# Quantised first-layer activations on VectorE, one of two ternary roundings on VectorE, a new order of the first norms and keys, and a last unit in halves

## The chip, the cores and the metric

The kernel runs on one core of a Trainium2 chip. The metric is the device time of one execution in microseconds; the time before is the median of three runs. A core has five engines with an instruction queue each: TensorE (PE in the views; PEld is its weight load), VectorE (DVE), ScalarE (ACT), GpSimd (POOL), and SyncE (SP), which here issues every DMA. An engine runs its queue in order; engines wait for each other through semaphores.

## What is computed

Two layers over 2 x 1024 tokens of width 256, each with gated cross-attention to 77 context rows (16 heads of 16) and a gated feed-forward part. In layer 0 the latter is ternary: activations are rounded to 8 bits, weights to -1, 0 or 1. In layer 1 the attention has a distance bias, and the feed-forward part is expert 0 of a mixture with a norm behind it.

```python
def _quant_act(x):
    scale = 127.0 / jnp.clip(jnp.max(jnp.abs(x), axis=-1, keepdims=True), EPS, None)
    xq = jnp.clip(jnp.round(x * scale), -128.0, 127.0) / scale
...
x = x + jnp.tanh(g_xattn[0]) * _L0_xattn_ref(_layernorm(x), ctx, w_q, w_k, w_v, w_o)
x = x + jnp.tanh(g_ffn[0]) * _L0_ffn_ref(_layernorm(x), w1, w2)      # _quant_act on x, and on gelu(h)
x = x + jnp.tanh(g_xattn[1]) * _L1_xattn_ref(_layernorm(x), ctx, ctx, distances, ...)
x = x + jnp.tanh(g_ffn[1]) * _L1_ffn_ref(_layernorm(x), ...)         # x + expert 0, normed
```

## The kernel before

The 2048 tokens are cut into 8 units (NU) of 256 rows; a tile holds a unit as 2 x 128 rows. Each engine's program is written out by hand as one function, so that its queue is the order of the code; semaphores (`then_inc`, `wait_ge`) tie the queues together. Two instructions that follow each other on VectorE or GpSimd with a dependence are tied by `link`.

**Start.** VectorE takes the statistics of units 0 and 1 (`ln0_stats`), norms them (`refine`, `ln0_apply`) and builds the key tables: `split_keys` makes high and low parts and the masked copies `km`, `keys_high` expands one (batch, half) of them to all heads (`kt_hi`, four calls). TensorE projects the keys (`tables_k`), transposes the normed units (`ln0_transposes`), projects queries (`queries`) and values (`tables_v`). SyncE loads inputs, then sends `km` into the tile `ktb` (`key_blocks`, three DMAs), then small rows of weights broadcast to all partitions (seven DMAs), then the query blocks and the shift rows of unit 0 into `qb`.

**Attention.** `attn_slot(l, s)` on each engine works on several units at once, in six steps r: maxima of the scores of unit s (`maxima` on TensorE, L1109 on VectorE), which end in the shift rows `mT` (L1522 on TensorE, L695 on ScalarE); scores, exponentials and their high parts on ScalarE (L704, L713) and low parts on GpSimd (`plo`, L491) for unit s-1; values for unit s-2; division, projection and residual for unit s-3; statistics (VectorE), factors (GpSimd, `factors_act`) and norm (ScalarE, L677) for unit s-4. In layer 0 unit s-4 is then quantised: `quantise` on VectorE (L1035 to L1042) takes the absolute maximum and its reciprocal at r = 4, just ahead of the last maximum of the slot, and `rounded` on ScalarE (L686) scales and rounds the unit at the end of the slot, just ahead of L695. Slots 0 to 3 also hold the first norms of the remaining units (`ln0_steps`, `ln0_applied`).

**Ternary stage.** Slots 9 to 12 of attention 0 also take ternary units 0 to 3; then follow ternary slots 4 to 8 alone, and 9 to 11 beside the first slots of attention 1. Per unit: a product to 1024 columns (L1600), gelu into the one buffer `h32` (L769), absolute maximum per half (L1155) and reciprocal (L1161) on VectorE, the rounding of the two halves of 128x1024 on ScalarE (L791, from `h32` to `hq`), transposes (L1615), their copies (L777), the second product (L1634), residual and statistics (L1178, L865), and GpSimd's norm (L431, L433, L517). The gelu of the next unit waits for both roundings. VectorE also builds the value tables of layer 1 here (`tables_v(1, step)`, L928 and L931, in slots 4 to 7) and the key tables (`keys_high(1, i)`).

**End.** `expert_hidden` and `expert_out` give a unit's sum in one PSUM bank; `expert_sum` adds and takes statistics on VectorE, GpSimd gives the factors, `expert_norm` (L1218, L1222) the output, which SyncE stores. GpSimd's queue per unit is: `xgb` (L527), `xnk` plus bias (L531, semaphore `xb`, which the sum waits for), factors.

## Time and profile before

| | us |
|---|---|
| runs | 415.22, 416.18, 414.89 (median 415.22) |
| profiled execution, its own time | 416.79 |
| its span, first to last instruction | 415.0 |
| TensorE busy / VectorE busy | 328.2 / 297.2 |
| ScalarE busy / GpSimd busy | 283.5 / 227.9 |

The span is that of one core; all times in the views count from its first instruction. Busy time is the union of an engine's instructions; waiting on a semaphore isn't counted, but an instruction that is held up after its issue by another engine is, so that its duration grows. The granted clock of TensorE is a share of 2.4 GHz, either 1.00 or 0.50 (1.2 GHz); in a stretch it is a mean.

### The profile page before, as it was taken

Reading aid. Unit: us, or ns where it says so; the run is one execution under the profiler, and the core shown is the slowest. Engines: PE = TensorE matmul, PEld = TensorE weight load, DVE = VectorE, ACT = ScalarE, POOL = GpSimd, SP = SyncE. Lnnn points to the kernel's source line nnn. Section 1 sums busy time; section 2 is a strip of 40 time slices with the busy share of each in tenths; the row PEclk is TensorE's granted clock in tenths of the full one; section 3 lists DMA queues with packets and bytes.
Section 4 is the critical chain, followed back from the end, with each engine's and each line's share of the span. In section 5 each row is a group of like instructions: output and inputs, shape, how many; then the busy total and the mean of one; then the engine's idle time right before and its main releaser. Section 6 shows DMA issues by size and latency. Waiting matters only on the chain.

```text
span 415.0 us, 8997 instructions
## 1 busy us (share of the span) xinstructions
PE 328.2 (79%) x3254; PEld 267.5 (64%) x3254; DVE 297.2 (72%) x690; ACT 283.5 (68%) x516; POOL 227.9 (55%) x408
## 2 busy tenths in 40 slices
PE   3658859787876765877787899898878899999990
PEld 2437648566664443455565788687667799888880
DVE  6685747877886657989986467777856558777775
ACT  4137787899896777988953788866678755555520
POOL 5246555776577411456766655567774155544442
PEclk9695898999899869869998999999999999999997
DMA  8996303111100000310073112211100000000001
GB/s 247 243 165 190 77 26 81 38 40 41 42 3 20 2 0 2 52 23 2 2 227 75 49 51 51 51 37 30 37 2 2 2 2 26 28 28 27 25 27 51
DMA packets 23171, 22.02 MB, mean 53 GB/s; under 512 B 4695, under 2 KB 22488, under 8 KB 23051
## 3 DMA queue, kind: packets, MB, share of 16 engines
q1 hardware_dynamic: 23128, 21.45, 20.9%
q8 instruction: 26, 0.43, 0.5%
q14 instruction: 17, 0.14, 0.1%
HBM read 10.34 MB, written 2.10 MB: 30 GB/s over the span
## 4 chain that ended last, share of the span: by engine, by line
PE 38%; DVE 26%; ACT 16%; issue 9%; POOL 8%; DMA 1%; SPq 0%; ACTq 0%; DVEq 0%; POOLq 0%
PE psA L1681 9%; PE psD L1666 4%; PE psBE L1666 4%; DVE st L865 4%; ACT pp_hi L713 3%; POOL lns L399 3%; DVE ham L1155 3%; PE psD L1370 3%; DVE mx L1109 3%; PE psA L1463 2%; ACT p L704 2%; PE psBE L1396 2%; PE psA L1634 2%; POOL pp_lo L491 1%; DVE o L1094 1%
## 5 line engine op out<-in xcount | busy, mean ns | idle before, releaser
L491 POOL TENSOR_TENSOR pp_lo<-p,pp_hi 124x512 f16<-124x512 f32 x80 | 92.7, 1178 | 45.6 <-ACT pp_hi L713 45.6
L399 POOL TENSOR_TENSOR lns<-lns,mhalf 128x2 f32<-128x2 f32 x40 | 32.2, 805 | 117.0 <-DVE lns L870 116.8
L1109 DVE TENSOR_REDUCE mx<-psBE 128x6 f32<-128x462 f32 (+1 forms) x96 | 54.6, 582 | 31.1 <-PE psBE L1396 30.8
L704 ACT ACTIVATE p<-psD 124x512 f32<-124x512 f32 x80 | 47.6, 597 | 28.7 <-PE psD L1370 26.1
L1370 PE MATMUL psD<-qb,ktb 98*124 98x256 f16 (+1 forms) x256 | 50.1, 293 | 5.7 <-DMA qb<-mT 4.8
L713 ACT ACTIVATE pp_hi<-p 124x512 f16<-124x512 f32 x80 | 50.4, 629 | 0.0
L1370 PEld LDWEIGHTS psD<-qb,ktb 98*124 98x124 f16 (+1 forms) x256 | 33.5, 147 | 10.5 <-DMA qb<-mT 6.8
L1396 PE MATMUL psBE<-kt_hi,q_hi 128*128 128x154 f16 (+2 forms) x160 | 34.2, 283 | 5.0 <-ACT mT L695 3.8
L1681 PE MATMUL psA<-ew_lo,pp_hi 128*128 128x256 f16 x128 | 34.9, 273 | 0.0
L1681 PE MATMUL psA<-ew_hi,pp_lo 128*128 128x256 f16 x128 | 34.9, 273 | 0.0
L1681 PE MATMUL psA<-ew_hi,pp_hi 128*128 128x256 f16 x128 | 34.9, 273 | 0.0
L1198 DVE TENSOR_TENSOR pp_lo<-space,pp_hi 128x512 f16<-128x512 f32 x32 | 23.4, 750 | 15.5 <-ACT space L815 15.4
L1422 PE MATMUL psA<-vo,pp_hi 124*128 124x34 f16 (+1 forms) x320 | 27.4, 181 | 8.8 <-ACT pp_hi L713 5.6
L1422 PEld LDWEIGHTS psA<-vo,pp_hi 124*128 124x128 f16 x320 | 25.4, 96 | 12.7 <-issue 12.4
L813 ACT ACTIVATE pp_hi<-psD,b1s 128x256 f16<-128x256 f32 x32 | 15.7, 490 | 19.8 <-PE psD L1666 19.8
L1425 PE MATMUL psA<-vo,pp_lo 124*128 124x34 f16 (+1 forms) x320 | 27.3, 181 | 0.0
L1424 PE MATMUL psA<-vlo,pp_hi 124*128 124x32 f16 (+1 forms) x320 | 27.3, 180 | 0.0
L865 DVE BATCH_NORM_STATS2 st<-xs 128x6 f32<-128x256 f32 x64 | 23.9, 415 | 2.3 <-DMA xs<-in_x 2.0
L1424 PEld LDWEIGHTS psA<-vlo,pp_hi 124*128 124x128 f16 x320 | 25.0, 96 | 0.4
L1425 PEld LDWEIGHTS psA<-vo,pp_lo 124*128 124x128 f16 x320 | 25.0, 96 | 0.0
L1367 PE MATMUL psD<-bb,selb 128*124 128x256 f16 x80 | 21.9, 284 | 1.2 <-DMA qb<-mT 1.1
L1396 PEld LDWEIGHTS psBE<-kt_hi,q_hi 128*128 128x128 f16 x160 | 15.3, 103 | 10.1 <-issue 4.6
(201 smaller groups left out, 1013.1 us busy)
## 6 DMA issues: line engine op xcount, KB each, us to landing
qb<-q_hi SPq DMA_DIRECT2D x32, 128.0 KB
xs<-in_x SPq DMA_DIRECT2D x8, 256.0 KB, 4.6
tw_raw<-in_tw SPq DMA_DIRECT2D x2, 1024.0 KB, 11.7
qb<-q_lo SPq DMA_DIRECT2D x16, 128.0 KB
space<-in_ew SPq DMA_DIRECT2D x2, 1024.0 KB, 6.5
out<-space SPq DMA_DIRECT2D x8, 256.0 KB, 2.1
ktb<-km SPq DMA_DIRECT2D x6, 248.0 KB, 9.4
qb<-bT_lo SPq DMA_DIRECT2D x8, 104.0 KB
```

The costliest lines, as they stand in the source:

```text
L399: nc.gpsimd.tensor_tensor(lns[:, n % 4, 1, :], lns[:, n % 4, 0, :], mhalf[:, :], ALU.pow).then_inc(s_rs, 1)
L491: nc.gpsimd.tensor_tensor(pl[:, u % 2, 2 * r:2 * r + 2, :], p32[:, n % 4, :, :], ph[:, u % 2, 2 * r:2 * r + 2, :], ALU.subtract).then_inc( ...
L704: a_(p32[:, n % 4, :, :], psD[n % 2][0:KR, :].rearrange("p (t r) -> p t r", t=2), ACT.Exp, scale=1.0 / SSC).then_inc(a["exp"], 1)
L713: a_(ph[:, u % 2, 2 * r:2 * r + 2, :], p32[:, n % 4, :, :], ACT.Copy).then_inc(a["phi"], 1)
L865: i = v.bn_stats(st[:, n % 4, j, :], src[:, j, :])
L1109: v.tensor_reduce(pairs[:, MP[k][0]:MP[k][1]:MP[k][2], :], psBE[:, n % 2, 0:hn * KEYS].rearrange("p (q e k) -> p q e k", e=2, k=KEYS), AX. ...
L1370: i = mm(o, ktbf[0:rows, block(g, hf * B + b, t):block(g, hf * B + b, t) + KR], qb[0:rows, u % NQ, g, hf, :], start=first, stop=(k == 1 an ...
L1396: i = mm(psBE[:, n % 2, o0 * KEYS:(o0 + c1 - c0) * KEYS], q[0][:, u % 2, hf, j * 128:(j + 1) * 128], kt[:, hf, b, c0 * KEYS:c1 * KEYS], st ...
L1422: mm(o, p_, w.rearrange("p s c -> p (s c)"), start=(hf == 0 and t == 0), stop=False, skip_group_check=True)
L1424: mm(ov[:, :, 0:HD], p_, wl, start=False, stop=False, skip_group_check=True)
L1425: i = mm(o, pl[:, u % 2, hf * TPH + t, rows_], w.rearrange("p s c -> p (s c)"), start=False, stop=(hf == 1 and t == TPH - 1), skip_group_c ...
L1681: i = mm(o, ehT[x_][:, u % 2, c, j * 128:(j + 1) * 128], ew2[w_][:, c, :], start=(j == 0 and c == 0 and x_ == 0 and w_ == 0), stop=(j == 1 ...
```

## The change

1. **Activations rounded by VectorE.** `rounded` on ScalarE goes. `quantise` rounds the unit by two instructions of 128x256 behind its reciprocal, ahead of the scales (`dq1`) and of the slot's last maximum.
2. **Ternary rounding.** Of the two halves, ScalarE keeps j = 0; VectorE does j = 1 (128x1024) in `ternary_first` behind the reciprocal, with a semaphore `q1b` of its own.
3. **Start.** On VectorE the head masks come first, both norms ahead of the keys, then two of four `keys_high`, then the masked copies (`keys_masked`, cut out of `split_keys`), the statistics of unit 2, and the low queries; the other two `keys_high` go to slots 2 and 3. TensorE projects queries 0 ahead of the transposes of unit 1. ScalarE spreads the query weights ahead of the key tables. SyncE sends the seven rows ahead of the key blocks.
4. **Layer-1 tables.** Value table steps go from ternary slots 4 to 7 to 7 to 10, without the column of ones (L931), which layer 0 has written; `keys_high(1, i)` for i = 1, 2, 3 go from slots 4, 5, 6 to 4, behind 9 and behind 10.
5. **End.** The last unit is summed, normed and stored in halves of 128 rows, the first half as soon as its product is done; its second half uses another PSUM bank.

VectorE at the start, from the first norm on; before:

```order
L884 TENSOR_SCALAR xn<-xs,mv,lns 128x256 x2
L958 TENSOR_REDUCE hmask<-id 128x8
L960 TENSOR_REDUCE pmask<-hmask 128x2
L896 CAST ksp_hi<-k 128x308
L897 TENSOR_TENSOR ksp_lo<-k,ksp_hi 128x308
L901 TENSOR_SCALAR km<-ksp_hi,pmask 128x4x77 x2
L901 TENSOR_SCALAR km<-ksp_lo,pmask 128x4x77 x2
L876 TENSOR_TENSOR lns<-lns 128x2
L877 TENSOR_TENSOR lns<-lns 128x2
L878 TENSOR_SCALAR lns<-lns 128x2
L879 TENSOR_TENSOR lns<-lns 128x2
L884 TENSOR_SCALAR xn<-xs,mv,lns 128x256 x2
```

after:

```order
L891 TENSOR_SCALAR xn<-xs,mv,lns 128x256 x2
L883 TENSOR_TENSOR lns<-lns 128x2
L884 TENSOR_TENSOR lns<-lns 128x2
L885 TENSOR_SCALAR lns<-lns 128x2
L886 TENSOR_TENSOR lns<-lns 128x2
L891 TENSOR_SCALAR xn<-xs,mv,lns 128x256 x2
L903 CAST ksp_hi<-k 128x308
L904 TENSOR_TENSOR ksp_lo<-k,ksp_hi 128x308
L921 TENSOR_TENSOR kt_hi<-ksp_hi,hmask 128x616 x2
L911 TENSOR_SCALAR km<-ksp_hi,pmask 128x4x77 x2
L911 TENSOR_SCALAR km<-ksp_lo,pmask 128x4x77 x2
L872 BN_STATS st<-xs 128x6 x2
```

The second norm (xn) stands ahead of the keys (ksp, kt_hi, km), and two expansions stand ahead of the masked copies.

VectorE in slot 4 of attention 0, the quantisation of unit 0; before:

```order
L1035 TENSOR_REDUCE am<-xn 128x2
L1037 TENSOR_SCALAR am<-am 128x1 x2
L1040 RECIPROCAL am<-am 128x2
L1042 TENSOR_SCALAR dq<-am,ws 128x1 x2
L1109 TENSOR_REDUCE mx<-psBE 128x2x2
L1079 SCALAR_TENSOR_TENSOR q_lo<-psA,q_hi 128x512
L1066 SCALAR_TENSOR_TENSOR xs<-psA,gsc,xs 128x512
```

after:

```order
L1048 TENSOR_REDUCE am<-xn 128x2
L1050 TENSOR_SCALAR am<-am 128x1 x2
L1052 RECIPROCAL am<-am 128x2
L1055 TENSOR_SCALAR xn<-xn,am 128x256 x2
L1058 TENSOR_SCALAR dq<-am,ws 128x1 x2
L1125 TENSOR_REDUCE mx<-psBE 128x2x2
L1095 SCALAR_TENSOR_TENSOR q_lo<-psA,q_hi 128x512
L1082 SCALAR_TENSOR_TENSOR xs<-psA,gsc,xs 128x512
```

Two instructions that round xn stand between the reciprocal and the last maximum of the slot.

VectorE at the end, from the sum of the unit before the last on; before:

```order
L1207 SCALAR_TENSOR_TENSOR space<-tw_raw,psA 128x512
L865 BN_STATS st<-space 128x6 x2
L868 BN_AGGR mv<-st 128x2 x2
L870 TENSOR_SCALAR lns<-mv 128x2
L1218 SCALAR_TENSOR_TENSOR space<-space,mv,bc 128x256 x2
L1222 SCALAR_TENSOR_TENSOR space<-space,lns 128x256 x2
L1207 SCALAR_TENSOR_TENSOR space<-tw_raw,psA 128x512
L865 BN_STATS st<-space 128x6 x2
L868 BN_AGGR mv<-st 128x2 x2
L870 TENSOR_SCALAR lns<-mv 128x2
L1218 SCALAR_TENSOR_TENSOR space<-space,mv,bc 128x256 x2
L1222 SCALAR_TENSOR_TENSOR space<-space,lns 128x256 x2
```

after:

```order
L1226 SCALAR_TENSOR_TENSOR space<-tw_raw,psA 128x512
L872 BN_STATS st<-space 128x6 x2
L875 BN_AGGR mv<-st 128x2 x2
L877 TENSOR_SCALAR lns<-mv 128x2
L1242 SCALAR_TENSOR_TENSOR space<-tw_raw,psA 128x256
L1243 BN_STATS st<-space 128x6
L1244 BN_AGGR mv<-st 128x2
L1245 TENSOR_SCALAR lns<-mv 128x1
L1264 SCALAR_TENSOR_TENSOR space<-space,mv,bc 128x256 x2
L1268 SCALAR_TENSOR_TENSOR space<-space,lns 128x256 x2
L1242 SCALAR_TENSOR_TENSOR space<-tw_raw,psA 128x256
L1243 BN_STATS st<-space 128x6
```

The first half-sum of the last unit stands ahead of the norm of the unit before it (two rows of space<-space), and the second behind it; the two half-norms follow.

The diff, cut to its core:

```diff
@@ -335,11 +335,11 @@
             sp.dma_start(tw1_raw[:, :, :], io["tw1"].rearrange("(c p) n -> p c n", p=128)).then_inc(d_tw1, 16)
-            key_blocks(0)
...
                 sp.dma_start(o, io[name].to_broadcast([128, o.shape[1]])).then_inc(d_row, 16)
+            key_blocks(0)
@@ -371,12 +371,16 @@
                 shift_rows(1, u)
-            for u in range(NU):
+            for u in range(NU - 1):
...
                              y32[:, u % 2, :, :]).then_inc(d_out[u % 2], 16)
-            for i in (0, 1):
-                sp.wait_ge(d_out[i], 16 * NU // 2)
+            u = NU - 1
+            for j in (0, 1):
+                sp.wait_ge(E["out"], u + 1 + j)
+                sp.dma_start(io["out"][u * UR + j * 128:u * UR + (j + 1) * 128, :], y32[:, 1, j, :]).then_inc(d_out[1], 16)
+            sp.wait_ge(d_out[0], 16 * NU // 2)
+            sp.wait_ge(d_out[1], 16 * (NU // 2 + 1))
@@ -424,6 +428,18 @@
+
+            def factors_half(j):
+
+                n = 5 * NU - 1
+                g = lns[:, n % 4, :, j:j + 1]
+                pool.wait_ge(s_var, n + 1 + j)
+                nc.gpsimd.tensor_tensor(g[:, 1, :], g[:, 0, :], mhalf[:, 0:1], ALU.pow).then_inc(s_rs, 1)
+                pool.wait_ge(s_rs, n + 1 + j)
+                link(nc.gpsimd.tensor_tensor(g[:, 2, :], g[:, 1, :], g[:, 1, :], ALU.mult))
+                link(nc.gpsimd.tensor_tensor(g[:, 3, :], g[:, 0, :], g[:, 2, :], ALU.mult))
+                link(nc.gpsimd.tensor_scalar(g[:, 4, :], g[:, 3, :], -0.5, 1.5, ALU.mult, ALU.add))
+                nc.gpsimd.tensor_tensor(g[:, 5, :], g[:, 4, :], g[:, 1, :], ALU.mult).then_inc(E["fac"], 1)
@@ -530,7 +546,10 @@
                                         orow[:, 1:2, :].to_broadcast([128, 2, D]), ALU.add).then_inc(E["xb"], 1)
-                factors_dve(4 * NU + u, E["fac"])
+                if u < NU - 1:
+                    factors_dve(4 * NU + u, E["fac"])
+            for j in (0, 1):
+                factors_half(j)
@@ -592,11 +611,10 @@
             keys_spread(0)
-            tables_k(0)
...
             a_(spreaded(wqp), spread(wraw[0, "q"]), ACT.Copy).then_inc(s_wqp, 1)
+            tables_k(0)
             ln0_transposed(0)
-            ln0_transposed(1)
@@ -747,8 +756,6 @@
                         expert_hidden(s - NU - 1, (r - 2, r - 1))
-                if l == 0 and 0 <= s - 4 < NU:
-                    rounded(s - 4)
@@ -784,12 +792,10 @@
                 if u < NU:
-                    for j in (0, 1):
-                        n = 2 * u + j
-                        act.wait_ge(f["amax"], u + 1)
-                        ge(act, f["phT"], n - 3)
-                        a_(hq[u % 2][:, j, :], h32[:, j, :], ACT.Identity, scale=ham[:, 2, j:j + 1],
-                           bias=epsc[:, 4:5]).then_inc(f["q1"], 1)
+                    act.wait_ge(f["amax"], u + 1)
+                    ge(act, f["phT"], 2 * u - 3)
+                    a_(hq[u % 2][:, 0, :], h32[:, 0, :], ACT.Identity, scale=ham[:, 2, 0:1],
+                       bias=epsc[:, 4:5]).then_inc(f["q1"], 1)
@@ -895,6 +902,9 @@
+
+            def keys_masked(l):
@@ -951,17 +962,19 @@
             v.memset(ktb[:, :, :, :].rearrange("p n g k -> p (n g k)").bitcast(F32), 0.0).then_inc(s_bm, 1)
-            ln0_stats(0)
-            ln0_stats(1)
-            ln0_apply(0, refine(0, SX))
...
             link(v.tensor_reduce(pmask[:, :], hmask[:, :].rearrange("p (g r) -> p r g", r=2), AX.X, ALU.max))
+            ln0_stats(0)
+            ln0_stats(1)
+            ln0_apply(0, refine(0, SX))
+            ln0_apply(1, refine(1, SX))
             split_keys(0)
-            ln0_apply(1, refine(1, SX))
-            for i in range(4):
+            for i in range(2):
                 keys_high(0, i)
+            keys_masked(0)
+            ln0_stats(2)
@@ -970,10 +983,10 @@
-                if (s, r) in ((0, 2), (0, 3), (0, 5), (1, 1), (1, 5), (2, 1)):
-                    ln0_stats({(0, 2): 2, (0, 3): 3, (0, 5): 4, (1, 1): 5, (1, 5): 6, (2, 1): 7}[s, r])
-                if (s, r) == (0, 1):
-                    queries_lo(0, 0)
+                if (s, r) in ((0, 2), (0, 5), (1, 1), (1, 5), (2, 1)):
+                    ln0_stats({(0, 2): 3, (0, 5): 4, (1, 1): 5, (1, 5): 6, (2, 1): 7}[s, r])
+                if (s, r) in ((2, 3), (3, 4)):
+                    keys_high(0, s)
@@ -1036,8 +1049,11 @@
                 link(i)
-                ge(dve, a["q1"], u)
                 v.reciprocal(am[:, 2, :], am[:, 1, :]).then_inc(a["xn"], 1)
+                dve.wait_ge(a["xn"], u + 1)
+                for j in (0, 1):
+                    i = v.tensor_scalar(xn[:, u % 2, j, :], xn[:, u % 2, j, :], am[:, 2, j:j + 1], MAGICQ, ALU.mult, ALU.add)
+                i.then_inc(a["q1"], 1)
@@ -1157,15 +1173,18 @@
                     link(i)
-                    ge(dve, f["q1"], 2 * u)
+                    ge(dve, f["q1"], u)
                     v.reciprocal(g[:, 2, :], g[:, 1, :]).then_inc(f["amax"], 1)
+                    dve.wait_ge(f["amax"], u + 1)
+                    ge(dve, f["phT"], 2 * u - 2)
+                    v.tensor_scalar(hq[u % 2][:, 1, :], h32[:, 1, :], g[:, 2, 1:2], MAGICQ, ALU.mult, ALU.add).then_inc(f["q1b"], 1)
...
                         v.tensor_scalar(dq2[:, n:n + 1], g[:, 1, j:j + 1], ws[:, 1:2], gate[:, 2:3], ALU.mult, ALU.mult)
-                if 4 <= s < 8:
-                    if s == 4:
+                if 7 <= s < 11:
+                    if s == 7:
                         dve.wait_ge(A[0]["ppv"], 2 * NU)
-                    tables_v(1, s - 3)
+                    tables_v(1, s - 6)
@@ -1209,6 +1228,33 @@
+            def expert_sum_half(j):
+                e, u = E, NU - 1
+                n = 4 * NU + u
+                y = y32[:, u % 2, j, :]
+                if j == 0:
+                    dve.wait_ge(e["half"], 1)
+                    dve.wait_ge(e["xb"], u + 1)
+                    dve.wait_ge(d_out[u % 2], 16 * (u // 2))
+                else:
+                    dve.wait_ge(e["pm2"], u + 1)
+                acc = acc_(u)[:, 0:D] if j == 0 else psX[:, D:2 * D]
+                link(v.scalar_tensor_tensor(y, xnk[:, 2 * u + j, :], SY / SX, acc, ALU.mult, ALU.add))
+                link(v.bn_stats(st[:, n % 4, j, :], y))
+                link(v.bn_aggr(mv[:, n % 4, j, :], st[:, n % 4, j, :]))
+                v.tensor_scalar(lns[:, n % 4, 0, j:j + 1], mv[:, n % 4, j, 1:2], EPS * SY * SY, None,
+                                ALU.add).then_inc(s_var, 1)
+
+            def expert_norm_half(j):
+                e, u = E, NU - 1
+                n = 4 * NU + u
+                y = y32[:, u % 2, j, :]
+                dve.wait_ge(e["fac"], u + 1 + j)
+                link(v.scalar_tensor_tensor(y, y, mv[:, n % 4, j, 0:1], gg[:, :], ALU.subtract, ALU.mult))
+                dve.wait_ge(e["xgb"], u + 1)
+                v.scalar_tensor_tensor(y, y, lns[:, n % 4, 5, j:j + 1], xgb[:, u % 2, j, :],
+                                       ALU.mult, ALU.add).then_inc(e["out"], 1)
@@ -1232,18 +1279,21 @@
                     split_keys(1)
+                    keys_masked(1)
...
                 ternary_slot(s)
-                if s < 7:
-                    keys_high(1, s - 3)
+                if s == 4:
+                    keys_high(1, 1)
...
             ternary_slot(NU + 1)
+            keys_high(1, 2)
...
             ternary_slot(NU + 2)
+            keys_high(1, 3)
@@ -1264,9 +1314,12 @@
                 expert_hidden(u, (2, 3))
-            for u in (NU - 2, NU - 1):
-                expert_sum(u)
-                expert_norm(u)
+            expert_sum(NU - 2)
+            expert_sum_half(0)
+            expert_norm(NU - 2)
+            expert_sum_half(1)
+            for j in (0, 1):
+                expert_norm_half(j)
@@ -1341,7 +1394,6 @@
             ln0_transposes(0)
-            ln0_transposes(1)
@@ -1637,8 +1689,8 @@
                     pe.wait_ge(f["xn"], u + 1)
-                    if u < 4:
-                        pe.wait_ge(s_vo, 8 + 2 * u + 1)
+                    if 3 <= u < 7:
+                        pe.wait_ge(s_vo, 8 + 2 * (u - 3) + 1)
@@ -1674,17 +1726,21 @@
                 ge(pe, e["y"], u - 1)
+                last = u == NU - 1
                 for j in (0, 1):
-                    o = acc_(u)[:, j * D:(j + 1) * D]
+                    o = (psX if last and j == 1 else acc_(u))[:, j * D:(j + 1) * D]
...
                             i = mm(o, ehT[x_][:, u % 2, c, j * 128:(j + 1) * 128], ew2[w_][:, c, :],
-                                   start=(j == 0 and c == 0 and x_ == 0 and w_ == 0),
-                                   stop=(j == 1 and c == FK - 1 and x_ == 1))
+                                   start=((last or j == 0) and c == 0 and x_ == 0 and w_ == 0),
+                                   stop=((last or j == 1) and c == FK - 1 and x_ == 1))
+                    if last and j == 0:
+                        i.then_inc(e["half"], 1)
...
             queries(0, 0)
+            ln0_transposes(1)
```

## Rows read from the trace of the kernel before

**Rows 1.** The page: span, and busy time, share of the span and instructions by engine.

```profile
span 415.0 us, 8997 instructions
PE 328.2 (79%) x3254; PEld 267.5 (64%) x3254; DVE 297.2 (72%) x690; ACT 283.5 (68%) x516; POOL 227.9 (55%) x408
```

**Rows 2.** Stretches: us, busy us (instructions) by engine, clock, DMA share, GB/s.

```profile
83.00:95.00 12.00, 10.11 (x131) 8.29 (x126) 9.10 (x24) 11.03 (x22) 8.74 (x13) 1.00 0.12 35
188.00:196.00 8.00, 5.98 (x62) 4.38 (x61) 7.83 (x21) 7.09 (x8) 5.23 (x9) 1.00 0.01 2
```

**Rows 3.** Timeline, 0 to 42 us: start, us, engine, line, operation, out<-in, [idle before <-releaser].

```profile
14.28 1.12 PE L1284 MATMUL psA<-id,xn 128*128 128x128 f32 x4 [4.13 <-DVE xn L884]
15.19 3.62 PE L1463 MATMUL psA<-xTf,ew_lo 128*128 128x256 f32 x8
21.51 1.19 DVE L1109 TENSOR_REDUCE mx<-psBE 128x6 f32<-128x462 f32 x2 [4.45 <-PE psBE L1396]
29.61 1.54 SPq L323 DMA_DIRECT2D qb<-mT  x2
33.18 0.85 PE L1370 MATMUL psD<-qb,ktb 98*124 98x256 f16 x3
```

**Rows 4.** DMA issues, first 60 us: KB each, median us to landing.

```profile
ktb<-km SPq DMA_DIRECT2D x3, 248.0 KB, 13.3
```

**Rows 5.** Stretches of 2 us in the start.

```profile
16.00:18.00 2.00, 2.00 (x6) 1.60 (x5) 1.07 (x2) 0.03 (x1) 0.00 (x0) 0.50 1.06 345
28.00:30.00 2.00, 1.14 (x9) 0.84 (x10) 1.63 (x5) 1.77 (x4) 1.59 (x6) 1.00 0.76 163
```

**Rows 6.** Timeline of ScalarE, slot 4 of layer 0.

```profile
79.22 1.09 ACT L677 ACTIVATE xn<-xs,lns 128x256 f32<-128x256 f32 x2 [1.36 <-POOL lns L416]
81.88 1.08 ACT L686 ACTIVATE xn<-xn,epsc,am 128x256 f32<-128x256 f32 x2
82.87 0.45 ACT L695 ACTIVATE mT<-psBE,epsc 16x256 f16<-16x256 f32 x1
```

**Rows 7.** Timeline of VectorE, the same slot.

```profile
80.34 0.69 DVE L1035 TENSOR_REDUCE am<-xn 128x2 f32<-128x512 f32 x1 [1.53 <-ACT xn L677]
81.62 0.47 DVE L1109 TENSOR_REDUCE mx<-psBE 128x4 f32<-128x308 f32 x1
```

**Rows 8.** Timeline of GpSimd, the same slot.

```profile
79.14 4.51 POOL L491 TENSOR_TENSOR pp_lo<-p,pp_hi 124x512 f16<-124x512 f32 x4
```

**Rows 9.** Timelines of GpSimd and VectorE, slot 3 of layer 0.

```profile
63.59 2.32 POOL L491 TENSOR_TENSOR pp_lo<-p,pp_hi 124x512 f16<-124x512 f32 x2 [0.77 <-ACT pp_hi L713]
...
63.88 1.02 DVE L996 TENSOR_SCALAR bc<-bc,gate 128x256 f32<-128x256 f32 x1
64.82 1.25 DVE L997 TENSOR_SCALAR bc<-bc,gate 128x256 f32<-128x256 f32 x1
70.07 0.34 DVE L999 TENSOR_SCALAR orow<-orow,gate 128x256 f32<-128x256 f32 x1
```

**Rows 10.** Timeline of VectorE, the fourth ternary unit.

```profile
172.48 2.35 DVE L1155 TENSOR_REDUCE ham<-space 128x1 f32<-128x1024 f32 x2 [0.63 <-ACT space L769]
```

**Rows 11.** Timelines of VectorE and GpSimd, ternary slots 4 and 5.

```profile
187.37 0.79 DVE L911 TENSOR_TENSOR kt_hi<-ksp_hi,hmask 128x616 f16<-128x616 f16 x1
191.77 0.80 DVE L931 TENSOR_SCALAR vo<-vm 124x15 f16<-124x15 f32 x1
...
191.24 1.27 POOL L517 TENSOR_TENSOR xs<-xs,orow 128x512 f32<-128x512 f32 x1
```

**Rows 12.** Timelines of TensorE and VectorE, ternary slots 6 and 9.

```profile
195.34 0.43 PE L1329 MATMUL psA<-vsp_hi,selb 77*124 77x48 f16 x5 [1.03 <-DVE xTf L890]
...
221.52 0.88 DVE L1178 SCALAR_TENSOR_TENSOR xs<-psA,dq,xs 128x256 f32<-128x256 f32 x2 [1.50 <-PE psA L1634]
```

**Rows 13.** Timelines of GpSimd and VectorE, the end.

```profile
404.71 1.44 POOL L531 TENSOR_TENSOR tw_raw<-tw_raw,orow 128x512 f32<-128x512 f32 x1
...
411.52 0.88 DVE L1222 SCALAR_TENSOR_TENSOR space<-space,lns 128x256 f32<-128x256 f32 x2
```

29 lines of the change are left out of this document (13 added, 16 removed).

## Prediction

> **What bounds the kernel now.** I read the page first: in a span of 415.0 us no engine is busy throughout; TensorE has 79%, VectorE 72%, ScalarE 68%, GpSimd 55% [rows 1]. So the price of an edit depends on its stage, and I read busy time by stretch, then the chain of work that ended last. In slot 5 of the first attention layer ScalarE works 11.03 of 12 us and VectorE 9.10; in ternary slots 5 and 6 VectorE works 7.83 of 8 us [rows 2]. There the timelines say who comes last. The experts of layer 1 (322 to 405 us) are a wall of TensorE work which the change leaves alone except for its last unit. The change acts in four places: the start, the first attention layer from slot 4 on, the ternary stage, and the end.
>
> **The start.** TensorE waits 4.13 us for the second norm before its transposes at 14.28, then does the first queries in 3.62 us, at half clock (granted 0.50, that is 1.2 GHz, after it had stood still; 1.00 is 2.4 GHz), and VectorE idles 4.45 us until the first maxima at 21.51 [rows 3, 5]. Now the queries stand before the second transposes, the second norm before the key tables, two of four key expansions are put off to slots 2 and 3 (VectorE idle there in the before trace), and one statistics step and the low queries stand ahead of slot 0. VectorE's list up to the first maximum then ends at about 16.5, and slot 0 starts some 5 us earlier. What is late next is the transfers. Today the first shift rows are sent at 29.61 and the first scores run at 33.18 [rows 3]. The scores also need the key blocks and the query blocks. The key blocks are now sent behind seven row transfers; today they take 13.3 us to land [rows 4], since the DMA engines are full to 28 us and still at 0.76 until 30 [rows 5]. The same bytes are queued ahead of the first scores in either order, so these can't start before about 30. That gains 33.2 - 30.2 = 3.0 us, plus about 0.3 for a wait on VectorE that has gone by then. **Term 1: -3.3** (bounds -4.8 and -1).
>
> **Rounding of the first-layer activations.** Per unit, ScalarE loses two instructions (1.08 us [rows 6]), and VectorE gets two of 128x256 between its reciprocal and the last maximum of the slot. Free, such an instruction takes 0.34 (L999, [rows 9]), the pair 0.65. In slot 4 the chain is: norm on ScalarE at 79.22, absolute maximum at 80.34, reciprocal ends at 81.5, last maximum at 81.62; the shift (L695) waits at 82.87 for the rounding in front of it [rows 6, 7]. Without other waits the new chain ends the last maximum at 82.75 and the shift starts near 83.1: +0.3. The ScalarE time that is freed is thus not gained, as VectorE's chain is nearly as long.
> But GpSimd then runs four subtractions in a row, 79.14 to 83.65, 1.13 each [rows 8]. Rows 9 show what happens to this very kind of instruction: L996 is issued at 63.88 and ends at 64.90, when the first of two GpSimd subtractions (63.59 to 65.91, a border near 64.75) is done; L997, right behind it, ends at 66.07, after the second. Each takes 0.29 to 0.34 when GpSimd is idle. So of a pair each instruction waits for one GpSimd operation. In slot 4 the first waits for 82.52, the second for 83.65: last maximum at 84.5, shift at 84.8, +1.9. The same reading gives +1.1 in slot 5, -0.55 in slot 6 (GpSimd's row has ended, ScalarE's relief counts), +1.9 in slot 7, where VectorE carries the chain, and +0.95 in slot 8, where part of the wait is only moved. Sum with waits +5.3; without any +1.0; if ScalarE's time came back in slots 5 and 6 as well, -1. I take a value near the upper end, as L996, L997 and L931, which meet a GpSimd operation, all wait for it [rows 9, 11]. **Term 2: +4.3** (-1 to +5.3).
> The Trainium skill, page "SBUF — State Buffer", section "Who interferes with whom", states that VectorE and GpSimd share a port pair as an exclusive lock: an instruction of VectorE in a two-port mode and one of GpSimd exclude each other, and the later one blocks fully until the other has ended. By that rule this term is the +5.3 and not the +1.0. The trace agrees: 1.25 us for L997 against 0.34 for L999.
>
> **Ternary rounding of the second half, slots 9 to 12.** One of two ScalarE roundings of 128x1024 goes to VectorE, about 0.75 free. In slot 9 the halves run beside each other and the unit's own new work is paid back (-0.3). In slot 10 the rounding stands before the statistics, whose GpSimd factors and ScalarE norm follow: about +1.0. In slot 11 VectorE has the activations' rounding and the half, 1.4 us, against 0.63 idle before its next maximum at 172.48 [rows 10]: another +0.8 to +1.0. In slot 12 VectorE has no gap at all: +0.75. **Term 3: +2.5** (0 to +4).
>
> **Ternary slots 4 to 8.** Here VectorE sets the pace [rows 2]. Taken off: in slots 4 to 6 the value tables (two of 0.32, and L931, which takes 0.80 because GpSimd's L517 runs from 191.24 to 192.51: 1.34 in all), in 5 and 6 also the key expansion, 0.71 net [rows 11]. Added: the half, 0.75 free to 1.8 behind a GpSimd operation; I take 1.35. That gives -1.0 in slot 4 (a gap of 0.86 goes too), -0.7 each in 5 and 6, +0.6 in 7, -0.1 in 8. **Term 4: -2.0** (-5 to -0.3).
>
> **Ternary slots 9 and 10, beside attention slots 0 and 1 of layer 1.** Two of the table steps land here: TensorE has 0.7 more (L1329, ten matmuls) ahead of a product for which VectorE already waits 1.50 us, and VectorE an expansion of 0.7 ahead of the next maxima [rows 11, 12]. Some is hidden by waits for transfers. **Term 5: +1.2** (0 to +2.5).
>
> **The end.** The last unit's sum, norm and output go in halves; half 0 is ready on TensorE 2.6 us before half 1. But the first half-sum needs GpSimd's L531 of the last unit, which ends at 404.71 + 1.44 = 406.15 [rows 13], behind the factors of the unit before. VectorE now waits there with that unit's norm queued behind it. From about 405.8: half-sum 1.15, norm 1.75 to 2.3, half-sum 1.15, factors 1.9, half-norm 0.9: VectorE ends at 412.4 to 413.1, today at 411.52 + 0.88 = 412.4 [rows 13]; the last transfer is half as large. **Term 6: +0.1** (-0.8 to +0.8).
>
> **Sum.** -3.3 + 4.3 + 2.5 - 2.0 + 1.2 + 0.1 = +2.8 us. The profiled execution took 416.79 (span 415.0 and 1.8 around it), 1.6 above the median; I put the difference on the median: 415.2 + 2.8 = **418.0**.
>
> **Rivals.** (a) *Balance.* The waits on GpSimd hit only about half of the roundings, since the shorter start shifts the phases, and ScalarE's relief counts in slots 5 and 6: term 2 is near +1.5, the sum 0.0: 415.2. For it: slot 6 meets no GpSimd work. Against: GpSimd's row starts with the factors that also release the norm, so both keep step. (b) *Faster.* The roundings don't wait (another operation and another tile than L996), term 2 +0.5, term 3 +1, term 4 -4, term 1 -4, the others +0.5 and 0: -6 at the far end, about -3.5 where half of that comes: 411.7. For it: the instructions at 76.5 and later that round weights take their free time; ScalarE loses some 2 us per unit where it is busiest. Against: rows 9. (c) *Clearly slower.* The key blocks, put behind seven transfers, land later than the queries and the shift rows: the start gains nothing from 30.2 on, the price is 3 us, and it decides if the first scores start after 33. Then 418.0 + 3.3 = 421.3. For it: 13.3 us to land. Against: the same bytes are ahead of the first scores anyway.
>
> **How the numbers follow.** Forecast 0.45 (own range 416.5 to 420), (a) 0.20, (b) 0.27, (c) 0.08. About 0.3%, or 1.25 us, is what a measurement of this kernel can tell from no change. Faster: (b) and an edge of (a), 0.29. Within: most of (a), 0.20. Slower: the forecast and (c), 0.51. The range 411.5 to 421.0 leaves out the far ends of (b) and (c).
>
> **What would show it.** First scores at 30 to 31 (term 1); each pair of the new 128x256 roundings spread over 1.5 to 2.3 us in slots 4, 5, 7 and 8, beside GpSimd's subtractions (term 2); ternary slots 5 and 6 near 7.0 us instead of 7.7 (term 4); VectorE idle for 3 to 4 us before the first half-sum (term 6). Pairs of 0.65 would refute term 2, and with it the sign.

## The result and the profile after

| | before | after |
|---|---|---|
| runs | 415.22, 416.18, 414.89, 414.37 | 427.6, 431.98, 427.48, 427.97 |
| median, us | 415.06 | 427.79 |
| profiled execution / its span | 416.79 / 415.0 | 427.6 / 425.8 |

The changed kernel is slower: ratio 1.033, 95% interval 1.026 to 1.040. The forecast was 418.0 (411.5 to 421.0): the sign was right, the size far too small. Of the executions behind all numbers below, four that were over 1.5% longer than the fastest of their kernel, at a low granted clock, are left out of medians and ratios: one of g1 (435.37), two of g3 (419.84, 416.42) and one of the kernel before (420.10). The rows below answer [rows 1, 2]: slot 5 is within a microsecond of its old place, ternary slots 5 and 6 begin five later.

```profile
span 425.8 us, 8995 instructions
PE 330.2 (78%) x3254; PEld 269.5 (63%) x3254; DVE 310.7 (73%) x712; ACT 267.4 (63%) x492; POOL 232.6 (55%) x413
...
83.00:95.00 12.00, 9.87 (x104) 8.06 (x103) 9.20 (x25) 9.93 (x19) 8.11 (x12) 0.94 0.16 35
193.00:201.00 8.00, 7.25 (x59) 5.04 (x58) 7.79 (x19) 6.35 (x8) 5.84 (x12) 0.96 0.01 2
```

VectorE is busy 13.5 us longer, ScalarE 16.1 less, and the span is 10.8 longer. In slot 5 ScalarE works 9.93 of 12 us instead of 11.03; in the ternary slots VectorE still works 7.79 of 8.

To see where, I compared the start of the same instruction in both traces. Each number is the delay against the profiled execution of the kernel before, in us; the right columns are experiments below (each named by its label's first part), which change the kernel before by one or two parts.

| moment | after | e5 round | f1 half | f2 tables | g4 half + tables | g3 start, no ones |
|---|---|---|---|---|---|---|
| shift rows, slot 3 | -3.3 | +0.6 | -0.5 | 0.0 | +0.6 | -1.5 |
| absolute maximum, slot 9 | +3.1 | +6.8 | -0.2 | +0.6 | +0.6 | -1.4 |
| residual, ternary unit 1 (slot 12) | +6.2 | +7.3 | +1.4 | +1.2 | +2.7 | -1.6 |
| residual, unit 5 (ternary slot 7) | +4.1 | +6.3 | +4.3 | -2.0 | +0.5 | -4.6 |
| residual, unit 6 (ternary slot 8) | +7.1 | +6.3 | +6.1 | +2.6 | +5.2 | -3.9 |
| shift rows, slot 2 of layer 1 | +10.6 | +6.3 | +4.8 | +6.1 | +8.6 | -5.2 |
| end of the span | +10.8 | +6.4 | +4.9 | +6.2 | +8.6 | -5.1 |

After slot 2 of layer 1 the delay stays the same to the end in every kernel: what is lost before it is never won back.

**Start.** The timeline of the changed kernel, which answers [rows 3]:

```profile
25.56 1.54 SPq L323 DMA_DIRECT2D qb<-mT  x2
...
30.95 0.90 PE L1422 MATMUL psD<-qb,ktb 98*124 98x256 f16 x3 [1.93 <-DMA qb<-mT]
```

The shift rows go out 4.1 us earlier, the first scores run 2.2 us earlier, and they wait for the landing of the shift rows, not of the key blocks (those take 8.8 us now).

**Activations' rounding.** Timeline of VectorE (and one row of GpSimd) in slots 4 to 8; L1055 is the new pair:

```profile
75.84 4.54 POOL L507 TENSOR_TENSOR pp_lo<-p,pp_hi 124x512 f16<-124x512 f32 x4
...
78.20 2.33 DVE L1055 TENSOR_SCALAR xn<-xn,am 128x256 f32<-128x256 f32 x2
...
92.81 0.67 DVE L1055 TENSOR_SCALAR xn<-xn,am 128x256 f32<-128x256 f32 x2
...
105.46 0.62 DVE L1055 TENSOR_SCALAR xn<-xn,am 128x256 f32<-128x256 f32 x2
...
116.91 2.33 DVE L1055 TENSOR_SCALAR xn<-xn,am 128x256 f32<-128x256 f32 x2
...
131.73 2.35 DVE L1055 TENSOR_SCALAR xn<-xn,am 128x256 f32<-128x256 f32 x2
```

Three pairs of eight are held up by 1.7 us; the others take their free 0.62 to 0.67. Within the first pair each instruction ends just behind one of GpSimd's borders, which lie 1.13 apart (75.84 + 3 x 1.13 = 79.24, + 4 x 1.13 = 80.38):

```profile
78.20 1.17 DVE L1055 TENSOR_SCALAR xn<-xn,am 128x256 f32<-128x256 f32 x1
...
79.30 1.24 DVE L1055 TENSOR_SCALAR xn<-xn,am 128x256 f32<-128x256 f32 x1
```

**Ternary slots 8 to 10 and the first slots of layer 1.** Timelines of TensorE and VectorE; L1382 are the table products, L1667 the transposes, L1686 the second product, L938 the table copies, L1337 the transposes of the norm:

```profile
207.04 0.44 PE L1382 MATMUL psA<-vsp_hi,selb 77*124 77x48 f16 x5 [4.80 <-DVE xTf L897]
...
214.96 0.43 PE L1382 MATMUL psA<-vsp_hi,selb 77*124 77x48 f16 x5 [2.20 <-DVE xTf L897]
...
215.51 1.05 PE L1667 MATMUL psA<-id,p 128*128 128x128 f16 x16
216.41 1.91 PE L1686 MATMUL psA<-ew_hi,wspace 128*128 128x256 f16 x16
...
214.12 0.69 DVE L897 TENSOR_TENSOR xTf<-psA,xTf 128x512 f16<-128x512 f32 x1
...
218.35 0.88 DVE L1197 SCALAR_TENSOR_TENSOR xs<-psA,dq,xs 128x256 f32<-128x256 f32 x2 [1.92 <-PE psA L1686]
...
242.15 0.40 DVE L938 TENSOR_TENSOR vlo<-psA,vm 124x240 f16<-124x240 f32 x1
...
242.65 0.63 PE L1337 MATMUL psA<-id,xn 128*128 128x128 f32 x4 [1.71 <-issue]
...
243.94 0.69 DVE L897 TENSOR_TENSOR xTf<-psA,xTf 128x512 f16<-128x512 f32 x1 [1.39 <-ACT xTf L580]
```

In the kernel before, ternary slot 8 had no table products, and its transposes ran as soon as ScalarE had rounded each half:

```profile
207.88 0.61 PE L1615 MATMUL psA<-id,p 128*128 128x128 f16 x8
208.80 0.62 PE L1615 MATMUL psA<-id,p 128*128 128x128 f16 x8 [0.31 <-ACT p L791]
209.26 1.91 PE L1634 MATMUL psA<-ew_hi,wspace 128*128 128x256 f16 x16
```

Its residual followed 3.28 us behind that of the unit before (207.93 to 211.21); now it is 6.28 (212.07 to 218.35). VectorE's half of unit 7 was rounded by 211.03 and ScalarE's by 212.15 (L797, 210.91 + 1.24), but the transposes start at 215.51: the table products stand ahead of them in the queue and wait, TensorE idle for 2.20 us, for VectorE's last copy (L897) out of the bank into which both the table products and the transposes of the norm go (psX). The slot thus runs through one chain, copy (L897), tables, transposes, ScalarE's copies, product, residual, where the kernel before had its transposes done by then.

**End.** VectorE, the last unit, answering [rows 13]:

```profile
411.95 0.17 DVE L877 TENSOR_SCALAR lns<-mv 128x2 f32<-128x2 f32 x1
416.50 0.42 DVE L1242 SCALAR_TENSOR_TENSOR space<-tw_raw,psA 128x256 f32<-128x256 f32 x1 [4.39 <-POOL tw_raw L547]
...
423.15 0.48 DVE L1255 SCALAR_TENSOR_TENSOR space<-space,lns 128x256 f32<-128x256 f32 x1
```

The idle time that the forecast named is there (4.39 us), and the end comes out even: +10.6 at slot 2, +10.8 at the end.

### The profile page after: what moved, and what is told of

Its sections match the earlier page's. It is cut to its first block, busy times and chain, and to the rows that moved or that the text cites. A ratio compares the mean times of both kernels' runs of the same rounds, so it can differ in the third digit from the quotient of the medians.

```text
span 425.8 us, 8995 instructions
## 1 busy us (share of the span) xinstructions
PE 330.2 (78%) x3254; PEld 269.5 (63%) x3254; DVE 310.7 (73%) x712; ACT 267.4 (63%) x492; POOL 232.6 (55%) x413
## 4 chain that ended last, share of the span: by engine, by line
PE 38%; DVE 30%; ACT 11%; issue 9%; POOL 8%; DMA 3%; SPq 1%; ACTq 0%; POOLq 0%; DVEq 0%
PE psA L1734 9%; PE psD L1718 4%; PE psBE L1718 4%; DVE ham L1171 4%; PE psD L1422 3%; DVE st L872 3%; DVE mx L1125 3%; ACT pp_hi L722 3%; POOL lns L403 2%; PE psA L1515 2%; DVE xn L1055 2%; PE psBE L1448 2%; DVE xs L1197 2%; PE psA L1520 2%; DMA qb<-mT 1%
## 5 line engine op out<-in xcount | busy, mean ns | idle before, releaser
L403 POOL TENSOR_TENSOR lns<-lns,mhalf 128x2 f32<-128x2 f32 x39 | 30.9, 792 | 110.7 <-DVE lns L877 110.5
L1422 PE MATMUL psD<-qb,ktb 98*124 98x256 f16 (+1 forms) x256 | 51.5, 301 | 5.4 <-DMA qb<-mT 4.7
L1422 PEld LDWEIGHTS psD<-qb,ktb 98*124 98x124 f16 (+1 forms) x256 | 33.9, 150 | 10.3 <-DMA qb<-mT 6.7
L819 ACT ACTIVATE pp_hi<-psD,b1s 128x256 f16<-128x256 f32 x32 | 15.7, 489 | 19.8 <-PE psD L1718 19.8
L1718 PE MATMUL psD<-xTf,ew_hi 128*128 128x256 f16 x128 | 21.4, 273 | 0.4 <-ACT p L713 0.4
```

Source lines behind the costliest of these rows:

```text
L403: nc.gpsimd.tensor_tensor(lns[:, n % 4, 1, :], lns[:, n % 4, 0, :], mhalf[:, :], ALU.pow).then_inc(s_rs, 1)
L1422: i = mm(o, ktbf[0:rows, block(g, hf * B + b, t):block(g, hf * B + b, t) + KR], qb[0:rows, u % NQ, g, hf, :], start=first, stop=(k == 1 an ...
L1718: i = mm(eps_(n)[:, i2 * UR:(i2 + 1) * UR], ew1[w_][:, k, c], x_[:, k, :], start=(i2 == 0 and k == 0 and x_ is xh and w_ == 0), stop=(i2 = ...
```

## The experiments

Ratios are to the kernel before on the same chip, with their 95% intervals. Runs were made in four groups, in which the median of the kernel before was 416.0, 417.5, 416.3 and 416.9, so I compare ratios, and delays of traces at the same instruction. "Part" is a part of the change.

### Undoing one part of the changed kernel

e3: part 4 undone, but L931 stays out. e2: part 2 undone. e1: part 1 undone.

```diff
 e3, TensorE (VectorE and keys_high likewise)
-                if 7 <= s < 11:
-                    tables_vo(1, s - 7)
+                if 4 <= s < 8:
+                    tables_vo(1, s - 4)
 e2, ScalarE rounds both halves
-                    v.tensor_scalar(hq[u % 2][:, 1, :], h32[:, 1, :], g[:, 2, 1:2], MAGICQ, ALU.mult, ALU.add).then_inc(f["q1b"], 1)
 e1, ScalarE
+                if l == 0 and 0 <= s - 4 < NU:
+                    rounded(s - 4)
```

> The changed kernel, with the value-table steps back in ternary slots 4 to 7 and the key expansions 1 to 3 of layer 1 back in slots 4 to 6 (the column of ones stays left out). Theory: in the changed kernel the table products stand on TensorE ahead of the transposes and the second product of ternary slots 7 to 10 and wait there for VectorE's copy of the norm before them (4.80, 2.20 and 0.28 us idle), and later the transposed norm waits for VectorE's table copies (242.65). That is the +6.5 between ternary slot 8 and attention slot 2 of layer 1. With the tables back this goes, and slots 4 to 6 pay about 1 to 2 us of VectorE's time again: 422.5 to 423.5, 4.5 to 5.5 under the changed kernel. Rival: the +6.5 is made by the rounding of the second half on VectorE (1.40 us at 209.63 instead of 0.75) and by what it pushes: then the tables' place matters little and the time stays at 427 to 429.

> The changed kernel, with both halves of the ternary rounding on ScalarE again. Theory: the rounding of the half costs 3 to 4 us, all in slots 9 to 12 of the first attention layer, where VectorE sets the pace; the time falls to 424 to 425. The +6.5 between ternary slot 8 and attention slot 2 of layer 1 stays. Rival: the half rounding is behind the +6.5 as well; then the time falls to 418 to 420.

> The changed kernel, with the rounding of the first-layer activations on ScalarE again. Theory: three of the eight pairs (slots 4, 7 and 8) stand still for 1.7 us each behind GpSimd's subtractions, and the pair in front of the last maxima costs some tenths in the other slots: the part costs 5 to 6 us, and the time falls to 422 to 423. Rival: other work takes the same places and only shifts the phases (the shorter start is given back anyway when the slots' phases move): the time falls by 2 us or less, to 426 or more.

Measured: e3 425.95, ratio 1.027 (1.020 to 1.034); e2 428.13, 1.033 (1.028 to 1.038); e1 423.62, 1.021 (1.015 to 1.028). All three expectations were put as if the parts were independent. e1 comes near, e2 gave nothing back, and e3 is split: two executions took 423.5 and 424.0 at a granted clock of 0.924, the changed kernel's own, near the 422.5 to 423.5 expected, and two, the profiled one among them, 427.9 and 429.0 at 0.914 and 0.915. In e1's trace the delay of the shift rows stays between -3.2 and -2.7 from slot 1 to slot 7, so what the changed kernel lost there (-3.7 to +1.9) is part 1's. In e3 the +3.0 of slot 8 is gone (+10.1 to +10.3), as the theory said, but slots 4 to 7 went from +7.5 to +10.1, where the changed kernel falls from +6.2 to +4.1. VectorE fills those slots without a gap; one of them, from one unit's absolute maximum at 196.09 to the next's at 204.11, is 8.0 us, against 7.1 in the changed kernel (199.66 to 206.81):

```profile
196.09 2.34 DVE L1171 TENSOR_REDUCE ham<-space 128x1 f32<-128x1024 f32 x2
...
198.92 0.92 DVE L1180 TENSOR_SCALAR p<-space,ham 128x1024 f32<-128x1024 f32 x1
...
203.40 0.79 DVE L921 TENSOR_TENSOR kt_hi<-ksp_hi,hmask 128x616 f16<-128x616 f16 x1
204.11 2.34 DVE L1171 TENSOR_REDUCE ham<-space 128x1 f32<-128x1024 f32 x2
```

So in slots 4 to 7 the half and the tables compete: with the tables back there, the half's time is paid in full. e2 shows no such filling. It gives back 2.0 us in slots 9 to 12 (+7.2 to +8.3, the changed kernel +3.1 to +6.2), its slots 4 to 7 fall from +8.3 to +6.1, as the changed kernel's do, and it loses in slot 8, +5.9, where its TensorE ran at half clock (0.50 from 217 to 223): from its table products to the end of the second product it took 6.35 us (216.87 to 223.22), and the changed kernel 3.36 at clock 1.00 (214.96 to 218.32). In attention slot 8 too, where neither part acts yet, e3 and e2 lose 3.2 and 3.5 us and the changed kernel 1.2; the granted clock from 120 to 140 us is 0.66 and 0.57 against 0.76. All four executions of e2 had a low clock (0.904 to 0.916; the changed kernel's four 0.916 to 0.924); whether that comes with this program or by chance is open. Undoing parts one by one didn't give their price; they had to be added one by one.

### One part alone on the kernel before

e4: part 3. e5: part 1. f1: part 2. f2: part 4. g4: parts 2 and 4. Their diffs are those lines of the change.

> The kernel before with only the new start (order of the first norms, keys, masks, queries, and of the row and key-block transfers). Theory: the gain at the first scores (3.3 us) is carried through to the end, since no later stage waits for a fixed moment: 411.5 to 412.5. Rival: the first attention layer gives part of it back (the two key expansions and the second copy of the norm now lie in slots 0 to 3, or other waits meet GpSimd's rows): 413.5 to 415.

> The kernel before with only the rounding of the first-layer activations moved to VectorE. Theory: the instructions stand still behind GpSimd's subtractions (up to 1.7 us for a pair, as at 78.20, 116.91 and 131.73 of the changed kernel, where a pair took 2.33 us instead of 0.62), and each pair delays the last maxima: 4 to 6 us, 419 to 421. Rival: the part costs its own 0.65 us per unit at most and often nothing; what was seen in the changed kernel came from the other parts: 415 to 417.

> The kernel before with only the second half of the ternary rounding moved to VectorE. The forecast's terms for it: +2.5 in slots 9 to 12, and about 1.35 us of VectorE's time per unit in ternary slots 4 to 8, where VectorE sets the pace, less what ScalarE's relief returns. Theory: with the table steps and the column of ones still in slots 4 to 7, the half comes on top of them in full: +2.5 and then 0.8 to 1.3 per slot, 421 to 424. Rival: the half is paid in slots 9 to 12 only and hidden later, since gelu and transposes of the next unit start earlier: 417 to 418.5.

> The kernel before with only the late layer-1 tables (value steps in ternary slots 7 to 10, expansions 2 and 3 behind slots 9 and 10, no column of ones). Theory: slots 4 to 6 get shorter by 0.7 to 0.9 each (VectorE sets the pace there), but from slot 8 on the table products stand ahead of the transposes on TensorE and wait for VectorE's copy of the norm, some 6 us in slot 8 and 9 when both roundings are ScalarE's, and 1 to 2 more where x transposes and the next maxima wait for the table copies and the expansion: 418 to 421. Rival: the late place is harmless when VectorE has no rounding to do, and the relief of slots 4 to 6 stays: 412.5 to 414.5.

> The kernel before with the second half of the ternary rounding on VectorE and the late layer-1 tables together (each alone cost 5.7 and 6.6 us). Theory: the table steps and expansions that leave slots 4 to 6 make room for the half there, and the half's halving of ScalarE's work shortens what waits behind the late tables in slots 8 and 9, so together they cost 6.5 to 8: 423 to 424.5. Rival: the costs are of different places and add up: 12 us, 427.5 to 429.

| | median | ratio, interval | part's cost, % |
|---|---|---|---|
| e4 start | 414.89 | 0.998 (0.995 to 1.002) | -0.2 |
| e5 rounding | 423.11 | 1.011 (1.006 to 1.015) | +1.1 |
| f1 half | 421.99 | 1.013 (1.008 to 1.017) | +1.3 |
| f2 tables | 422.93 | 1.014 (1.009 to 1.020) | +1.4 |
| g4 half and tables | 425.14 | 1.019 (1.017 to 1.022) | +1.9 |

e4 took its rival's time (413.5 to 415), not the 411.5 to 412.5 of the theory: its first scores come at 32.36, 0.8 earlier instead of 3, and its trace ends 2.0 earlier. e5's time is above the 419 to 421 expected, but in a group where the kernel before took 417.5; the cost of 4 to 6 held, by the median (5.6) and by the trace: pairs of 2.33 in slots 4, 7 and 8, and +6.2 between slot 3 and slot 9. f1's held: +2.9 of its delay arises in slots 4 to 7. For f2 I gave 418 to 421; it took 422.9, more than its rival and more than the theory. The relief in slots 4 to 7 is real (+1.2 to -2.0), and 8.1 us are lost behind it: 4.6 in slot 8, 3.5 until slot 2 of layer 1. Of the 4.6, a part is TensorE's clock, which in f2 fell to 0.51 and 0.64 from 209 to 213; the same transposes and product take 1.05 and 1.91 us in the changed kernel:

```profile
209.71 1.88 PE L1618 MATMUL psA<-id,p 128*128 128x128 f16 x16
211.38 2.44 PE L1637 MATMUL psA<-ew_hi,wspace 128*128 128x256 f16 x16
```

From the table products to the end of the second product f2 takes 4.99 us and g4, which loses 4.7 in this slot, 5.01 (clock 0.73 and 0.50 from 211 to 215), where the changed kernel takes 3.36. Less this difference, slot 8 costs 3.0 in f2, in g4 and in the changed kernel alike (in e2, too, 5.9 less 3.0 is 2.9).

g4 is between the theory (6.5 to 8) and the sum (12): 8.2 by medians. The two overlap by about 4.1 us by medians (8.2 against 5.7 + 6.6) and by 2.5 in the traces (8.6 against 4.9 + 6.2), where f1's lacks a half clock of 1.6 us that the others have between slots 0 and 1 of layer 1 (see the last section). 1.9 of it is in slots 4 to 7 (g4 -2.2 there, f1 and f2 together +2.9 - 3.2 = -0.3), 1.7 in slot 8 (g4 +4.7, f1 and f2 together +1.8 + 4.6). So the late tables do make room for the half, as the change seems to want, but they cost more later than they give. The parts now add up: start -2.0, rounding +6.4, half and tables +8.6, less 1.6 of half clock in g4's slot 8, are +11.4 by the traces, against +10.8; by ratios -0.2 + 1.1 + 1.9 = +2.8%, against +3.3 (2.6 to 4.0).

### The wait on GpSimd: form and size of the instruction

e6 writes the rounding with a second tensor operand, f4 cuts each rounding in two; both on e5.

```diff
 e6
-                    i = v.tensor_scalar(xn[:, u % 2, j, :], xn[:, u % 2, j, :], am[:, 2, j:j + 1], MAGICQ, ALU.mult, ALU.add)
+                    i = v.scalar_tensor_tensor(xn[:, u % 2, j, :], xn[:, u % 2, j, :], am[:, 2, j:j + 1],
+                                               epsc[:, 4:5].to_broadcast([128, D]), ALU.mult, ALU.add)
 f4
+                    for h in (0, 1):
+                        xq = xn[:, u % 2, j, h * 128:(h + 1) * 128]
+                        i = v.tensor_scalar(xq, xq, am[:, 2, j:j + 1], MAGICQ, ALU.mult, ALU.add)
```

> As the run before, but each rounding is written as one instruction with a second tensor operand (a broadcast constant, scalar_tensor_tensor instead of tensor_scalar). Theory: L1197, an instruction of this form and size, takes 0.44 us wherever GpSimd works beside it, so it is only the form with one tensor operand that is held up; each pair takes 0.9 us everywhere, none above 1.1, and the part costs 1.5 to 2.5 us: 416.5 to 418. Rival: every instruction of VectorE that comes then is held up (or slowed by the traffic): pairs of 2 us and more show as before, and the time is that of the run before or longer.

> The kernel before with the rounding of the first-layer activations on VectorE, each 128x256 instruction cut into two of 128x128 (same elements, four instructions instead of two). Theory: an instruction of this kind waits until the GpSimd operation in progress has ended, whatever its own size; four of them beside a row of GpSimd subtractions take up to four such waits, 3.4 to 4.6 us instead of 2.33 in slot 4, 7 and 8, and the time grows by 2 to 5 us: 425 to 428. Rival: the two engines share a rate, so the time goes with the elements: 2.4 to 2.7 us for the four, and 423 to 424.

e6 took 426.69, 1.021 (1.015 to 1.027); f4 427.55, 1.026 (1.019 to 1.033). e6's theory fell: the pair takes 2.60 us in slot 4 and 0.88 where it is free, so it is held up by the same 1.7.

```profile
81.54 2.60 DVE L1031 SCALAR_TENSOR_TENSOR xn<-xn,am,epsc 128x256 f32<-128x256 f32 x2
...
149.39 0.88 DVE L1031 SCALAR_TENSOR_TENSOR xn<-xn,am,epsc 128x256 f32<-128x256 f32 x2
```

L1197, on which I had built it, has this form too, but one of its operands lies in PSUM; here is its group in the changed kernel (min, median and max in ns), GpSimd working beside nine of the sixteen:

```profile
L1197 DVE SCALAR_TENSOR_TENSOR xs<-psA,dq,xs x16: 467/473/484, 173.2 to 229.6; 128x256 f32<-128x256 f32 x16
```

So the name of the operation doesn't tell whether it waits: with both tensor operands in SBUF it did, with one of them in PSUM it didn't. e6 took 3.6 us more than e5. The Trainium skill, page "SBUF — State Buffer", section "Who interferes with whom", states that an instruction of VectorE with two inputs in SBUF contends with a GpSimd instruction that reads SBUF, and one with at most one such input outside the two-port modes doesn't; the trace agrees with both halves, 2.60 against 0.88 us and 467 to 484 ns. That sentence stands beside the one that the prediction used.

f4 settles the price. GpSimd's row of four subtractions here runs from 78.77 to 83.27, with borders near 79.9, 81.0 and 82.1; VectorE's four quarters:

```profile
81.14 1.10 DVE L1033 TENSOR_SCALAR xn<-xn,am 128x128 f32<-128x128 f32 x1
...
82.16 1.19 DVE L1033 TENSOR_SCALAR xn<-xn,am 128x128 f32<-128x128 f32 x1
...
83.27 0.47 DVE L1033 TENSOR_SCALAR xn<-xn,am 128x128 f32<-128x128 f32 x2
```

The first two wait for one GpSimd operation each and take about as long as the full ones (1.17 and 1.24), at half the size; then the row ends and the other two are free. I had expected four waits, 3.4 to 4.6 us, and forgotten the row's end: 2.6. The time still went up, by 4.4 against e5's median (two runs only, and in another group: by ratios 1.5%), in the trace by 2.8; slot 5, where the pair had slipped through in 0.80, now takes 1.83.

### The late tables: order in TensorE's queue

e7 is the changed kernel with the table products behind the transposes; g1 is the changed kernel with the old start, g2 both.

```diff
+                ternary_transposed(s - 1)
                 if 7 <= s < 11:
                     tables_vo(1, s - 7)
-                ternary_transposed(s - 1)
```

> The changed kernel, with the value-table products of layer 1 behind the transposes of the same ternary slot on TensorE instead of ahead of them (slots 7 to 10). Theory: in slot 9 the transposes wait in the queue behind the table products, which wait until VectorE has copied the norm out of the same bank; without that the second product comes some 2 to 3 us earlier: 424.5 to 426. Rival: the transposes would wait for ScalarE or for the rounding anyway, and VectorE then waits for the tables instead, ahead of its residual: 427 to 429.

> The changed kernel with the start of the kernel before. Theory: all that the start gained, at its first scores, is lost again, no more: 1.5 to 3.5 us above the changed kernel, 429 to 431. Rival: the new start shifts phases against GpSimd's rows and is itself behind a part of the loss: below 428.

> As the run before, with the value-table products of layer 1 behind the transposes of the same ternary slot on TensorE instead of ahead of them. Theory: the transposes and the second product of slots 8 and 9, and the transposed norm in attention slot 2 of layer 1, come 2 to 3 us earlier in all: 2 to 3 us below the run before. Rival: no difference in time, since VectorE then waits for the tables in the same slots.

e7 427.45, 1.022 (1.016 to 1.028); g1 429.3, 1.030 (1.027 to 1.032); g2 428.51, 1.026 (1.023 to 1.029). e7's time is its rival's (427 to 429), though its ratio lies below the changed kernel's 1.033, with intervals that overlap. g2 is 0.8 below g1 by medians, with intervals that touch: the expected 2 to 3 us aren't there. In the traces slot 8 costs 2.1 instead of 3.0 in both pairs (e7 against the changed kernel, g2 against g1), so the order is a third of it. The rest stays, since the second product still stands behind the tables, which wait for the copy of the norm (e7):

```profile
215.30 1.06 PE L1667 MATMUL psA<-id,p 128*128 128x128 f16 x16
217.53 0.43 PE L1382 MATMUL psA<-vsp_hi,selb 77*124 77x48 f16 x5 [1.18 <-DVE xTf L897]
...
218.09 1.91 PE L1686 MATMUL psA<-ew_hi,wspace 128*128 128x256 f16 x16
```

That another bank would free it is argued from these waits; it wasn't tried. Much of each pair's remaining difference is the clock's. From the shift rows of slot 0 to those of slot 1 of layer 1, e7 and g1, whose TensorE stayed at 1.00, both take 12.3 us, and the changed kernel and g2, which fell to 0.50 (235 to 237, and 235 to 241), take 14.0 and 15.2. So e7, whose shift rows of slot 3 come 2.7 later than the changed kernel's, ends level with it (+10.9), and g2 ends 2.5 behind g1. g1's median is 1.5 above the changed kernel's 427.8, the low edge of its theory, but by ratios it is no higher (1.030 against 1.033), so these runs don't show what the start is worth there. Its rival, below 428, fell: the losses didn't grow from the new start.

### What is left when nothing moves onto VectorE

e8 and, once more in more rounds, g3: part 3 and the missing column of ones. f3 adds part 5.

```diff
-                i.then_inc(s_vo, 1)
-                v.tensor_scalar(vo[:, b, hf, :, :, HD], vm[:, :, :], SM * SONE, None, ALU.mult).then_inc(s_vo, 1)
+                i.then_inc(s_vo, 1 + l)
+                if l == 0:
+                    v.tensor_scalar(vo[:, b, hf, :, :, HD], vm[:, :, :], SM * SONE, None, ALU.mult).then_inc(s_vo, 1)
```

> The kernel before with the new start, and without the column of ones of the layer-1 value tables (L931, four times in ternary slots 4 to 7, 0.35 to 0.80 us each on VectorE), which layer 0 has written. Theory: VectorE sets the pace there, so the column's 1.5 to 3 us come off, on top of the start's 1.5: 411 to 412.5. Rival: VectorE then waits for TensorE's second product instead: 413.5 to 415.

> The kernel before with the new start, no column of ones in layer 1, and the end in halves: the three parts that moved no work onto VectorE. Theory: start 1.5 to 3, column 1 to 2, end nothing: 412 to 414, as without the halves at the end. Rival: the shorter last transfer and the earlier first half take 0.5 to 1.5 us off at the end: 411 to 412.

> The kernel before with the new start and no column of ones in layer 1, once more and in more rounds. Theory: 1.5 to 3.5 us under the kernel before, as in the first measurement of it (3.6 by medians). Rival: the first measurement met a fast transfer in the start, and the gain is within 1.3 us, as with the halves at the end added (0.8 by medians).

e8 413.96, 0.988 (0.981 to 0.995); g3 411.2, 0.987 (0.984 to 0.989); f3 415.55, 0.995 (0.992 to 0.999). The first two agree by ratio, and this version beats both kernels: 1.3% faster than the one before. By microseconds e8 lies in its rival's range, g3 gains more than its theory (5.7 by medians), and f3 is above both of its ranges. The column's place shows in g3's delays (-1.6 at unit 1, -4.6 at unit 5: 3.0 us in four ternary slots); e4, where the column stays, gains 0.8 over the same slots, so about 2 of the 3.0 are the column's. f3's smaller gain isn't explained by its end, whose length is the same in e8 and f3 within 0.2 us (15.5 and 15.7 from the sum of the unit before the last to the end of the span); its trace loses 1.7 us in slots 9 to 12, ahead of the added part, and 2.5 more from unit 5 to slot 2 of layer 1 (-3.1 to -0.6), where its TensorE fell to 0.50 twice (215 to 217 and 225 to 227). Its twelve executions have granted clocks of 0.923 to 0.938, the four of g3 0.938 to 0.943. So part of the gap may be the clock's; why is open.

## Why the prediction was wrong, by its terms

Term by term, the delay in the changed kernel's trace against the forecast:

| term | forecast | measured | from |
|---|---|---|---|
| 1 start | -3.3 | -3.3 | slot 3 |
| 2 activations' rounding | +4.3 (-1 to +5.3) | +6.4 | slot 3 to slot 9 |
| 3 half, slots 9 to 12 | +2.5 (0 to +4) | +3.1 | slot 9 to unit 1 |
| 4 ternary slots 4 to 8 | -2.0 (-5 to -0.3) | +0.9 | unit 1 to unit 6 |
| 5 slots 9, 10 beside attention | +1.2 (0 to +2.5) | +3.5 | unit 6 to slot 2 |
| 6 end | +0.1 | +0.2 | slot 2 to the end |
| sum | +2.8 | +10.8 | |

**Term 1: size right in this execution, by luck in part, and one reason wrong.** The first scores start at 30.95, as said, but that is 2.2 us earlier, where the working had 3.0. But it isn't the key blocks that are late next, it is the shift rows themselves, 4 KB sent into full queues. Rival (c) falls: the key blocks land in 8.8 us. Its price is not firm either: first scores at 30.89 to 33.83 in the programs with the new start, and e4, the start alone, gained only 0.2% (-0.5 to +0.2).

**Term 2: the mechanism right, the size cut without cause.** The waits came, one GpSimd operation each (f4), and the form with a second operand in SBUF doesn't escape them (e6). The working had +5.3; I took +4.3 "near the upper end", and the measured +6.4 is above it. By slot it is +2.4, +0.8, -0.3, +2.3 and +1.2, against +1.9, +1.1, -0.55, +1.9 and +0.95. In slot 5 the pair was not held up (0.67) and cost its own time all the same. In slot 4 the last maximum ends where the working had it (its 84.5, less the 3.3 of the start, is 81.2; it ends at 81.16), but from there to the shift it allowed 0.3 us, and there are 0.78, since the transposes of the maxima stand between:

```profile
81.22 0.69 PE L1574 MATMUL psBE<-id,mx 128*128 128x128 f32 x2 [2.09 <-DVE mx L1125]
```

TensorE had stood still for 2.09 us behind VectorE's chain, and its granted clock is 0.76 from 80 to 82 and 0.50 from 82 to 84. In slot 7 it is the same (0.69 for the transposes, 0.79 in all); in slots 5 and 6 they take 0.44 and the way to the shift 0.53. That accounts for the 0.5 and 0.4 by which slots 4 and 7 exceed the working; in e5, where the transposes of slot 4 took 0.44, the slot cost 2.1. Rival (a) was near in its count (three pairs of eight were held up, and none in slots 5 and 6), but it needed ScalarE's relief to pay in slots 5 and 6, and they brought +0.8 and -0.3. Rival (b) needed roundings that don't wait.

**Term 3** was 0.6 short, within its bounds.

**Term 4: the failed step is the last of its list, "-0.1 in 8".** Slots 4 to 7 gave -2.1, where the list has -1.0 - 0.7 - 0.7 + 0.6 = -1.8. Slot 8 cost +3.0. I had priced the table step that lands there by its busy time on VectorE, and not asked what its products on TensorE wait for and what stands behind them there; yet [rows 12] shows such a wait of 1.03 us for the same copy in slot 6. In slots 4 to 7 of the kernel before that wait was covered, because VectorE set the pace; in slot 8, where no new unit's maxima fill VectorE, the same wait is on the path. f2 shows it alone: +4.6 in slot 8, 3.0 without its half clock.

**Term 5** failed by the same step: 0.7 on each engine was counted, but not the round trip. In slot 2 of layer 1 the transposes of the norm (242.65) wait for the table copies, which stand behind VectorE's low queries (the view names no releaser for them; the kernel has them wait for the semaphore of these copies, and they start 0.1 us behind the last), and VectorE then waits 1.39 us for the copy of these transposes, with the expansion of 0.79 behind it. This slot brings 2.2 of the 3.5.

**Term 6** was right, with its mechanism (4.39 us idle).

2.1 + 0.6 + 2.9 + 2.3 = 7.9 of the 8.0 that the sum was short. The rest up to the median's 9.8 is the reference: the profiled execution of before lay 1.7 above its median, that of after 0.2 below.

## What to carry over

When a step is moved to another slot, write down for each of its instructions what it waits for and what stands behind it in that queue, there and not where it came from; a wait that was free under one engine's full load is paid in the first slot that isn't full. A rounding on VectorE beside GpSimd's subtractions waits for one GpSimd operation, whatever its size; additions with an operand in PSUM (L1197) didn't, nor did the absolute maxima, which read SBUF alone (L1171, 1.21 us each with GpSimd at work or not). Where GpSimd works in rows, a 0.65 us pair is 2.33. Two parts that use the same gap can't be priced by taking one of them away; add them one at a time. And before a delay of one trace is put down to an edit, compare the durations of the matmuls in that stretch: slot 8 read as 3.0, 4.6, 4.7 and 5.9 us in four programs, and was 3.0 with the clock taken out.

## What was not expected of the hardware

The same program ran through the same place at both levels of TensorE's clock. e8 and g3 have the same text; these are stretches of 2 us (columns as in [rows 2]) around the first queries of layer 1, e8 first, then g3:

```profile
207.00:209.00 2.00, 1.07 (x9) 0.49 (x7) 1.93 (x7) 0.84 (x2) 2.00 (x2) 1.00 1.00 384
209.00:211.00 2.00, 1.18 (x8) 0.37 (x6) 1.91 (x4) 0.00 (x0) 1.61 (x6) 0.95 1.09 366
211.00:213.00 2.00, 2.00 (x11) 1.45 (x10) 0.64 (x1) 0.00 (x0) 1.90 (x2) 0.50 1.18 208
```

```profile
209.00:211.00 2.00, 1.06 (x7) 0.47 (x6) 1.93 (x7) 0.84 (x2) 2.00 (x3) 1.00 1.00 374
211.00:213.00 2.00, 1.18 (x8) 0.62 (x9) 1.80 (x5) 0.00 (x0) 1.59 (x6) 1.00 1.09 366
213.00:215.00 2.00, 1.81 (x17) 1.27 (x14) 0.93 (x2) 0.82 (x2) 1.92 (x3) 1.00 1.17 174
```

TensorE had done the same before (1.07 and 1.18 of 2 us busy, 1.06 and 1.18), and fell to 0.50 (1.2 GHz) in one execution and not in the other. With a second fall at 221 to 225, e8 lost 2.5 us between unit 5 and slot 2 of layer 1 (-6.3 to -3.8), and g3 gained 0.6 (-4.6 to -5.2): 3.1 us, for which the clock is the only cause that these rows offer. Such a difference is as large as terms 1 and 3 of this prediction.

One stretch gives the price, from the shift rows of slot 0 to those of slot 1 of layer 1, in the 18 traces of this case:

| | clock 1.00 | one fall to 0.50 | longer at 0.50 |
|---|---|---|---|
| tables early | 11.1 to 11.2 us (f1, g3, e3) | 12.6 to 12.8 (before, e4, e5, e6, e8, f3, f4) | |
| tables late | 12.3 (e2, e7, g1) | 14.0 (after, e1, f2, g4) | 15.2 (g2) |

In this stretch late tables cost 1.1 to 1.4 us and the first fall 1.4 to 1.8, whatever else the program changes: when one trace is compared with another, the clock weighs as much as the edit.

The landing of the shift rows differed too: sent at 24.23 in e4 and 25.56 in the changed kernel, they let the first scores start at 32.36 and 30.95. The earlier sent landed later, while the queues were full (share 0.81 to 1.05 from 24 to 34 us in the changed kernel).
